# Who stores the expert results: ScalarE's own queue in place of SyncE's, and new places for every queue

## The chip, the cores and the metric

The kernel runs on one core of a Trainium2 chip. The metric is device time in microseconds (us) for one execution of the whole program, inputs in HBM to output in HBM; three executions are behind the median given below.

## The reference

32 sequences of 512 tokens of width 256 go through one Mamba block and its MLP, a layer norm, and then a mixture of 8 experts plus a shared one; a second layer norm ends it. What matters here is the last part:

```python
scores = softmax(xf @ gate_w.T);  _, idx = top_k(scores, 2)
weights = take_along_axis(scores, idx, -1)
y = per expert: (silu(x @ wg.T) * (x @ wu.T)) @ wd.T
routed = sum over a token's two experts of weight * y
out = layernorm(x + routed + shared(x))
```

## The kernel before

**Batches and engines.** The program walks over 32 batches (one sequence each) and three more periods, `b` in the code. Every engine works through one list of instructions in order. In a batch the Mamba scan takes most of the time: VectorE (DVE) runs 64 scans (L1224), ScalarE (ACT) makes the decay factors for each of them two ahead, into two PSUM banks (L750), GpSimd (POOL) multiplies their inputs (L585) and TensorE (PE) transposes their results (L969), which DVE sums with weights (L1240). Around this run the preparation of the next batch (`pre`), and the gate, the MLP and the shared expert of the batch before (`post`).

**Routed rows.** GpSimd scatters each token's row, with its weight as a 257th element, to two places in the HBM table `X_slots`, so that rows of one expert lie together. When a group of batches (6, 6, 6, 6, 4, 2, 1, 1) is complete, DVE works out a table `where` in SBUF: for each tile of 128 rows the row number it begins at and the expert. Two tiles make a pair; pairs 0 to 151 are spread over batches 5 to 30, in 12 slots per batch: 5 or 4 pairs in a batch at first, then 7, 10 and 12, and 8 in batch 30. The last group's 8 pairs have their own code, `last`.

**One pair's way.** SyncE (SP) loads the two experts' weights into `wx[k]` and the rows into `xin[k]`, with k the pair's number modulo 2 (L480 to L490). PE transposes the rows (L1107), ACT copies them out (L837), PE multiplies (L1125), ACT takes a tanh (L842), DVE makes the hidden values (L1368, L1371), PE multiplies again (L1140), and ACT scales the two result tiles into `xin[k]` (L853). Then SP stores both to `Y_slots` at the same row numbers. Before each DMA whose address depends on the data, SP reads the number with `value_load`:

```python
sp.wait_ge(s_yo, (p + 1) * 2)                     # ACT wrote both results of pair p
if before[g] >= 0: sp.wait_ge(s_gathered, ...)    # the table's former rows were read
for i in range(2):
    r = sp.value_load(where[g % 2][0:1, 0, tile + i:tile + i + 1], ...)
    sp.dma_start(Y_slots[g % 2][bass.ds(r, P), :], xin[k][:, i, 0:D]).then_inc(s_Y_out[k], 16)
```

The loads of pair p wait for `s_Y_out[k]` of pair p-2, since they write the same buffers. `finish` later gathers from `Y_slots` for each batch (POOL, L642), normalises it (ACT) and stores it.

**The order.** On each engine the strands (scan, pre, post, experts, results, finish and so on) are generators. `weave` merges them by a written table of places, `AT`: a step of batch b stands at 64 b plus its entry, and the lowest is issued next. SP's strands are the batches' inputs, `B_rows` (L409), the broadcasts `Bbc` for the scan (`B_spread`, L418, four buffers, each waiting until GpSimd is done with its former content), `experts` (the loads), `results` (the stores), `finish` and `last`.

Of the kernel before, what the change touches and what calls it, by code (L numbers as in the profile page):

```python
# [9 lines left out]
def group_sizes(n):  # L10
# [6 lines left out]
    while n:  # L17
# [4 lines left out]
AT = {  # L22
    "ACT_clear": [58.23, 58.23, 58.25, 58.25, 60.69, 60.69, 62.42, 62.42, 62.86, 70.07, 91.79, 94.81, 94.81, 95.76,
        95.89, 96.2, 101.55, 101.55, 101.55],
    "ACT_experts": [124.75, 125.75, 129.08, 130.18, 134.55, 136.08, 137.89, 139.34, 141.67, 141.67, 144.29, 145.62,
        147.34, 149.08, 152.77, 153.29, 159.33, 160.04, 160.86, 162.05, 166.89, 167.48, 170.25, 171.88],
    "ACT_finish": [152.64, 152.64, 152.64, 152.79, 153.07, 153.12, 153.36, 153.36, 155.18, 155.73, 156.96, 157.93,
        167.33, 167.33, 167.96, 167.96, 167.96, 168.52, 168.52, 168.91, 170.14, 170.82, 170.93, 171.03, 193.37,
        193.51, 193.51, 193.86, 199.66, 199.99, 199.99, 199.99, 200.21, 200.21, 200.21, 200.21],
    "ACT_last": [136.01, 137.58, 138.23, 138.31, 138.43, 138.43, 138.43, 138.43, 140, 140.51, 140.51, 142.7, 142.7,  # L30
        142.7, 142.7, 142.7, 143.93, 143.93, 143.93, 143.93, 143.93, 144.04, 144.04, 144.04, 144.04, 147.88, 148.81,
        148.81, 152.33, 154.88, 164.02, 167.57],
    "ACT_post": [59.67, 59.67, 64.96, 69.44, 79.33, 80.25, 80.77, 80.77, 82.16, 82.16, 82.16, 82.16, 82.8, 83.44,
        83.44, 84.7, 85.35, 85.71, 87.26, 87.56, 88.85, 90.21, 97.47, 97.47, 98.66, 98.69, 99.97, 101.17, 102.57,
        102.89, 104.72, 105.69, 109.85],
    "ACT_pre": [-61.77, -61.77, -61.77, -58.5, -58.31, -58.31, -49.46, -48.98, -47.21, -33.7, -33.7, -32.82, -32.38,
        -32.27, -30.87, -25.5, -23.6, -20.88, -19.14, -17, -13.55, -12.39, -10.98, -7.68, -5.62, -2.35],
    "ACT_results": [127.98, 128.73, 131.12, 131.93, 137.03, 137.03, 140.85, 141.1, 143.74, 143.74, 146.2, 146.61,
        150.27, 150.3, 158.46, 158.66, 160.18, 160.83, 165.45, 165.85, 168.76, 169.32, 172.65, 172.65],
    "ACT_scan": [2.32, 2.32, 6.33, 8, 8, 8.52, 8.78, 9.17, 9.17, 10.82, 12.09, 12.09, 14.29, 14.29, 15.76, 15.83,  # L40
# [3 lines left out]
    "ACT_weigh": [8.76, 9.09, 10.64, 11.74, 34.98, 36.17, 36.53, 37.63],  # L44
    "DVE_experts": [127.17, 129.69, 136.27, 139.69, 144.39, 148.41, 149.45, 153.29, 161.06, 162.66, 169.85, 175.15],
    "DVE_last": [129.08, 140.77, 140.77, 140.77, 153.53, 153.53, 158.09, 203.9],
    "DVE_meta": [108.09, 109.36, 110.61, 111.98],
    "DVE_post": [57.6, 62.15, 65.02, 68.32, 69.12, 73.9, 75.44, 75.44, 93.47, 97.9, 98, 98, 98.02, 102.46, 104.09,
        104.09, 104.74, 104.74, 104.98, 105, 105.13, 106.39, 107.33, 108.88],
    "DVE_pre": [-29.64, -26.56, -26.56, -25.13, -25.03, -23.53, -20.37, -19.9, -19.9, -18.38, -18.38, -18.38],  # L50
    "DVE_scan": [3.32, 3.48, 6.82, 7.53, 8.29, 8.29, 8.38, 10.1, 10.7, 11.64, 14.78, 14.86, 17.75, 19.56, 20.14,
# [4 lines left out]
    "DVE_weigh": [16.36, 17.6, 17.6, 19.63, 20.54, 20.54, 20.54, 20.54, 20.54, 20.54, 20.54, 22.81, 23.36, 23.36,  # L56
# [3 lines left out]
    "PE_experts": [122.03, 123.93, 126.2, 128.38, 135.99, 135.99, 139.17, 139.31, 141.28, 141.28, 146.72, 146.82,  # L60
        149.57, 149.57, 152.77, 152.77, 159.71, 161.24, 164.33, 164.59, 168.56, 168.83, 173.68, 174.09],
    "PE_inputs": [121.91, 125.67, 133.2, 137.49, 140.56, 145.8, 148.99, 152.41, 158.77, 164.23, 168.28, 170.67],
    "PE_last": [128.18, 128.18, 128.18, 130.61, 144, 144, 144, 154.96, 160.84, 161.21, 198.92, 198.92, 198.92,
        198.92, 222.27, 247.75, 247.75, 336.97, 357.99, 357.99, 357.99, 357.99, 357.99, 370.12],
    "PE_post": [55.43, 56.65, 56.65, 57.47, 58.38, 59.94, 61.6, 66.95, 67.63, 69.63, 73.15, 74.6, 75.44, 75.98,
        77.21, 79.8, 81.28, 81.6, 81.6, 81.74, 86.07, 86.07, 86.84, 86.84, 86.84, 86.84, 88.16, 88.52, 88.87, 88.87,
        90.27, 90.7, 90.98, 93.38, 93.38, 98.19, 99.97, 100.05, 100.95, 100.99, 102.79, 104.52, 104.52, 105.96,
        106.05, 106.16, 106.26, 109],
# [20 lines left out]
    "SP_experts": [110.03, 122.95, 127.33, 133.34, 144.56, 147.72, 148.88, 158.4, 159.99, 163.15, 164.6, 166.33],
    "SP_finish": [139.78, 160.64, 169.44],  # L90
    "SP_inputs": [-67.65],
    "SP_last": [105.48, 105.79, 115.27, 119.17, 119.17, 119.17, 119.17, 119.29, 119.29, 120.53, 135.17, 135.17,
        135.52, 135.52, 135.52, 147.56, 147.56, 147.56, 147.56, 159.42, 159.42, 159.42, 159.42, 159.42],
# [22 lines left out]
def build(nc, a, out):  # L116
    F32, BF16 = mybir.dt.float32, mybir.dt.bfloat16
    ALU = mybir.AluOpType
    ACT = mybir.ActivationFunctionType
# [61 lines left out]
    with ctx:  # L181
# [199 lines left out]
        def _(sp):  # L381
# [110 lines left out]
            def results():  # L492
                for b in range(PERIODS):
                    for p in pairs_in[b]:
                        if p is None:
                            yield from empty(b, 1)
                            continue
# [977 lines left out]
```

## Time and profile before

| | us |
|---|---|
| median of 3 runs | 5452.79 (5439.62 to 5469.59) |
| the profiled execution | 5453.14 |
| its span on the core | 5451.4 |
| DVE, PE, POOL, ACT busy in the span | 4418.7, 4273.5, 3581.1, 3392.8 |
| granted TensorE clock, mean share of full speed | 0.91 |

"Busy" counts instructions that compute; waits, register instructions and the issue of DMAs are not in it. A row of the timeline gives the start, the duration and, in brackets, how long the engine had been idle before and what ended that. A line that ends in q (SPq, ACTq) is the engine's sequencer, which issues DMAs; "x2" says that two like instructions in a row were merged.

### The profile page before, as it was taken

The page shows a single profiled execution, that of the slowest core. Times are in us where ns is not written, and L with a number is a line of the kernel's source. Part 1 is how long each engine was busy: PE and PEld are TensorE (multiplying, and loading weights), DVE is VectorE, ACT ScalarE, POOL GpSimd, SP SyncE. Part 2 cuts the span into 40 slices and gives each one's busy share as a digit, 9 for nine tenths or more (in the row PEclk, how much of TensorE's full clock was granted, in tenths as well). Part 3 has the DMA queues.
Part 4 walks back from the last instruction along what each step waited for, and adds up shares of the span by engine and source line. Part 5 has one row for each costly group of instructions (what it writes and reads, how often), then busy time and mean ns, then how long its engine had stood idle before and what let it go on. Part 6 is the DMA issues. An engine that isn't in the chain of part 4 may idle for free. (4 is left out here: it accounts for less than half of the span.)

```text
span 5451.4 us, 75865 instructions
## 1 busy us (share of the span) xinstructions
PE 4273.5 (78%) x20928; PEld 2954.8 (54%) x20928; DVE 4418.7 (81%) x6313; ACT 3392.8 (62%) x6338; POOL 3581.1 (66%) x2252
## 2 busy tenths in 40 slices
PE   3777877788888888878887778888878888888873
PEld 2455555455555555555555555555555566555652
DVE  5889988978888887788888788788888888878741
ACT  4666666556666656666666666666667776667633
POOL 4666666656566566666677666677767785677743
PEclk7898898999899999899999899899999999988987
DMA  1122522233333333332332332333334442455555
GB/s 57 61 76 80 136 81 79 81 101 116 107 127 111 107 92 98 89 104 84 88 95 77 97 103 84 87 92 89 94 110 113 125 132 88 141 141 145 155 141 152
DMA packets 357156, 563.53 MB, mean 103 GB/s; under 512 B 40433, under 2 KB 203378, under 8 KB 356610
## 3 DMA queue, kind: packets, MB, share of 16 engines
q1 hardware_dynamic: 253250, 398.07, 24.4%
q0 software_dynamic: 49152, 67.27, 6.1%
q10 hardware_dynamic: 54336, 93.34, 5.1%
q8 instruction: 174, 2.85, 0.2%
q14 instruction: 244, 2.00, 0.1%
HBM read 440.66 MB, written 186.05 MB: 115 GB/s over the span
## 5 line engine op out<-in xcount | busy, mean ns | idle before, releaser
L585 POOL TENSOR_TENSOR dBx<-dtx,Bbc 128x1024 f32<-128x1024 f32 x1024 | 2424.0, 2397 | 749.3 <-DVE hs L1224 721.5
L1224 DVE TENSOR_TENSOR_SCAN hs<-ps,dBx 128x512 f32<-128x512 f32 x2048 | 2397.8, 1208 | 179.7 <-ACT ps L750 132.9
L750 ACT ACTIVATE ps<-dt,A 128x512 f32<-128x512 f32 x2048 | 1389.4, 690 | 598.4 <-DVE hs L1224 538.5
L969 PE MATMUL ps<-ident,hs 128*128 128x128 f32 x8192 | 1325.6, 302 | 366.4 <-DVE acc L1240 186.7
L969 PEld LDWEIGHTS ps<-ident,hs 128*128 128x128 f32 x8192 | 1037.7, 154 | 858.8 <-issue 408.2
L1240 DVE SCALAR_TENSOR_TENSOR acc<-ps,C_tok,acc 128x512 f32<-128x512 f32 x1792 | 1282.0, 740 | 237.1 <-PE ps L969 218.6
L642 POOL DMA_INDIRECT fx<-Y_slots,slots x256 | 403.8, 1577 | 124.8 <-issue 56.7
L618 POOL DMA_INDIRECT X_slots<-xs,slots x256 | 257.1, 1004 | 323.4 <-DVE slots L1356 264.4
L1125 PE MATMUL ps<-xsT,wx 128*128 128x128 f32 x2432 | 339.8, 293 | 99.1 <-ACT xsT L837 99.1
L1125 PEld LDWEIGHTS ps<-xsT,wx 128*128 128x128 f32 x2432 | 317.0, 207 | 130.5 <-issue 127.6
L1213 DVE SCALAR_TENSOR_TENSOR xc<-ps,conv_w,xc 128x511 f32<-128x511 f32 (+2 forms) x384 | 285.5, 744 | 74.3 <-ACT xc L714 65.9
L934 PE MATMUL ps<-xnT,w_in 128*128 128x512 f32 x512 | 274.9, 654 | 75.5 <-DVE xc L1213 74.7
L1368 DVE SCALAR_TENSOR_TENSOR ge<-ge,ps 128x256 f32<-128x256 f32 x152 | 63.4, 417 | 325.2 <-ACT ge L842 322.1
L986 PE MATMUL ps<-xnT,w_in 128*128 128x512 f32 x512 | 316.1, 715 | 0.0
L569 POOL TENSOR_TENSOR dt<-dt,dtx 128x1024 f32<-128x1024 f32 x64 | 152.2, 2378 | 197.4 <-ACT dtx L741 197.4
L1016 PE MATMUL ps<-w_out,xc 128*128 128x256 f32 x1024 | 259.9, 391 | 0.0
L1049 PE MATMUL ps<-w_m,post_tmp 128*128 128x256 f32 x1024 | 252.1, 379 | 0.0
L1032 PE MATMUL ps<-mT,w_m 128*128 128x512 f32 x512 | 240.2, 602 | 15.1 <-ACT mT L793 10.6
L714 ACT ACTIVATE xc<-ps,conv_b,conv_w 128x512 f32<-128x512 f32 x128 | 99.0, 774 | 218.8 <-PE ps L934 216.8
L1140 PE MATMUL ps<-wx,ge 128*128 128x256 f32 x608 | 178.1, 418 | 66.8 <-DVE ge L1371 64.6
L958 PE MATMUL ps<-few 16*128 16x512 f32 x256 | 188.3, 826 | 52.4 <-DVE hs L1224 27.1
L837 ACT ACTIVATE xsT<-ps 128x512 f32<-128x512 f32 x152 | 90.0, 592 | 205.4 <-PE ps L1107 203.0
(210 smaller groups left out, 6090.3 us busy)
## 6 DMA issues: line engine op xcount, KB each, us to landing
Bbc<-B_scratch SPq DMA_DIRECT2D x512, 256.0 KB
wx<-in_experts SPq DMA_DIRECT2D x308, 384.0 KB, 5.3
Y_slots<-zeros ACTq DMA_DIRECT2D x228, 256.0 KB, 3.6
xin<-X_slots SPq DMA_DIRECT2D x308, 128.5 KB, 4.1
Y_slots<-xin SPq DMA_DIRECT2D x308, 128.0 KB
xt<-in_x SPq DMA_DIRECT2D x32, 512.0 KB, 5.6
shared<-xt ACTq DMA_DIRECT2D x32, 512.0 KB
fx<-shared SPq DMA_DIRECT2D x32, 512.0 KB
```

What stands on the lines that cost most here:

```text
L585: pool.tensor_tensor(dBx[u % 3][:], dtx[b % 2][:, 2 * h:2 * h + 2, :], Bbc[g % NBB][:, n % CH:n % CH + 1, :].broadcast_to([P, 2, T]), ALU. ...
L618: pool.indirect_dma_start(out=X_slots[g % 2], out_offset=bass.IndirectOffsetOnAxis(ap=slots[:, b % NKEPT, c, t:t + 1], axis=0), in_=xs[:, ...
L642: pool.indirect_dma_start(out=fx[:, t, :], out_offset=None, in_=Y_slots[g % 2], in_offset=bass.IndirectOffsetOnAxis(ap=slots[:, f % NKEPT, ...
L750: act.activation(psA[s % 2][:], dt[b % 2][:, j, :], ACT.Exp, scale=A[:, j, n:n + 1]).then_inc(s_dA, 1)
L934: i = pe.matmul(bank(b, j)[:], w_in[:, k, j * P:(j + 1) * P], xn[:, k, :], start=(k == 0), stop=(k == KD - 1))
L969: i = pe.transpose(psH[w % 2][:, j * P:(j + 1) * P], hs[(n * CT + j) % NHB][:, t * P:(t + 1) * P], ident[:])
L986: i = pe.matmul(psG[j % 2][:], w_in[:, k, DI + j * P:DI + (j + 1) * P], xn[:, k, :], start=(k == 0), stop=(k == KD - 1))
L1016: i = pe.matmul(psG[q][:, t * D:(t + 1) * D], c[:, k, (2 * q + t) * P:(2 * q + t + 1) * P], w_out[:, k, :], start=False, stop=(k == CT - 1))
L1125: i = pe.matmul(psE[:, o * HALF + m * P:o * HALF + (m + 1) * P], w[:, m, (2 * k + o) * P:(2 * k + o + 1) * P], xsT[:, (m * KD + k) * P:(m ...
L1213: dve.scalar_tensor_tensor(out=c[:, j, s:], in0=bank(b, j)[:, 0:T - s], scalar=conv_w[:, j, NK - 1 - s:NK - s], in1=c[:, j, s:], op0=ALU.m ...
L1224: dve.tensor_tensor_scan(hs[s % NHB][:], psA[s % 2][:], dBx[s // 2 % 3][:, s % 2, :], 0.0, ALU.mult, ALU.add).then_inc(s_scan, 1)
L1240: dve.scalar_tensor_tensor(out=o, in0=psH[w % 2][:], scalar=C_tok[b % 2][:, t, n:n + 1], in1=o, op0=ALU.mult, op1=ALU.add).then_inc(s_weig ...
```

## The change

SP's strand `results` is gone. ACT's strand `results` gets a third step for each pair, in which it waits for its own two result tiles, for the gathers and for the table `where`, reads both row numbers and issues both stores on its own DMA queue:

```diff
@@ sync @@
-            def results():
-                ...
-                        sp.wait_ge(s_yo, (p + 1) * 2)
-                        if before[g] >= 0:
-                            sp.wait_ge(s_gathered, gathers(first[before[g]] + groups[before[g]] - 1))
-                        for i in range(2):
-                            r = sp.value_load(where[g % 2][0:1, 0, tile + i:tile + i + 1], min_val=0, max_val=ROWS - P)
-                            sp.dma_start(Y_slots[g % 2][bass.ds(r, P), :], xin[k][:, i, 0:D]).then_inc(
-                                s_Y_out[k], 16)
...
@@ scalar, results @@
                         for i in range(2):
                             yield b
                             act.wait_ge(s_down_e, p + 1)
-                            act.activation(xin[p % 2][:, i, 0:D], psE[:, i * D:(i + 1) * D], ACT.Copy,
-                                           scale=xin[p % 2][:, i, D:ROW]).then_inc(s_yo, 1)
+                            act.activation(xin[k][:, i, 0:D], psE[:, i * D:(i + 1) * D], ACT.Copy,
+                                           scale=xin[k][:, i, D:ROW]).then_inc(s_yo, 1)
+                        yield b
+                        act.wait_ge(s_yo, (p + 1) * 2)
+                        if before[g] >= 0:
+                            act.wait_ge(s_gathered, gathers(first[before[g]] + groups[before[g]] - 1))
+                        act.wait_ge(s_meta, (g + 1) * NMETA)
+                        for i in range(2):
+                            r = act.value_load(where[g % 2][0:1, 0, tile + i:tile + i + 1], min_val=0, max_val=ROWS - P)
+                            act.dma_start(Y_slots[g % 2][bass.ds(r, P), :], xin[k][:, i, 0:D]).then_inc(s_Y_out[k], 16)
```

Nearly every entry of `AT` is another number, mostly by less than one place in 64. Those that the prediction speaks of (the twelve slots of a batch are the columns; ACT's results now have three entries per slot):

```diff
-    "SP_experts": [110.03, 122.95, 127.33, 133.34, 144.56, 147.72, 148.88, 158.4, 159.99, 163.15, 164.6, 166.33],
-    "SP_results": [124.93, 132.24, 136.86, 145.2, 147.75, 154.41, 158.46, 160.8, 163.86, 164.62, 168.83, 176.47],
+    "SP_experts": [106.86, 108.87, 130.44, 135.81, 143.11, 145.05, 145.81, 150.54, 154.74, 161.01, 161.01, 161.01],
-    "ACT_results": [127.98, 128.73, 131.12, 131.93, 137.03, 137.03, 140.85, 141.1, 143.74, 143.74, 146.2, 146.61,
...
+    "ACT_results": [128.79, 128.88, 129.17, 131.79, 132.06, 134.08, 136.96, 136.96, 137.26, 139.83, 140.55, 140.55,
+        143.32, 143.48, 143.48, 145.66, 146.04, 146.52, 150.26, 150.9, 152.4, 158.66, 158.66, 159.11, 160.25, 160.53,
...
-    "SP_B_spread": [-5.78, -4.69, -4.69, -2.74, 8.16, 8.16, 21.1, 21.46, 22.74, 35.01, 35.03, 35.6, 36.9, 38.27,
-        39.5, 42.35],
+    "SP_B_spread": [-13.16, -2.29, 0.35, 1.28, 10.17, 16.9, 22.83, 22.83, 23.43, 27.24, 27.56, 28.23, 34.68, 34.68,
+        42.58, 42.58],
```

## Rows read from the trace of the kernel before

**Rows 1.** The page: busy us, share of the span, instructions.
```profile
PE 4273.5 (78%) x20928; PEld 2954.8 (54%) x20928; DVE 4418.7 (81%) x6313; ACT 3392.8 (62%) x6338; POOL 3581.1 (66%) x2252
```

**Rows 2.** Timeline: once a batch, the store of its rows (batches 1, 2, 11, 12).
```profile
467.41 0.34 ACTq L825 DMA_DIRECT2D shared<-xt  x1
...
614.35 0.33 ACTq L825 DMA_DIRECT2D shared<-xt  x1
...
2199.07 0.33 ACTq L825 DMA_DIRECT2D shared<-xt  x1
...
2368.04 0.33 ACTq L825 DMA_DIRECT2D shared<-xt  x1
```

**Rows 3.** Waits of the whole span: who for whom, us, times, longest.
```profile
DVE ge L1368 <- ACT ge L842: 322.1, 102, 17.6
...
DVE hs L1224 <- ACT ps L750: 132.9, 176, 4.9
...
PE ps L1107 <- DMA xin<-X_slots: 116.0, 50, 6.4
```

**Rows 4.** Waits of SP's queue, the same columns.
```profile
SPq L505 <- ACT xin L853: 1798.8, 146, 29.8
...
SPq L486 <- DMA Y_slots<-xin: 33.9, 23, 3.2
```

**Rows 5.** Timeline of SP's queue after the second pair of batch 12.
```profile
2257.91 1.82 SPq L506 DMA_DIRECT2D Y_slots<-xin  x2
2259.84 0.37 SPq L519 DMA_DIRECT2D fx<-shared  x1
2261.66 0.35 SPq L488 DMA_DIRECT2D wx<-in_experts  x1
...
2264.37 0.33 SPq L490 DMA_DIRECT2D xin<-X_slots  x1
```

**Rows 6.** Timeline: the third pair of batch 12 on its engines.
```profile
2268.88 1.11 PE L1107 MATMUL ps<-ident,xin 128*128 128x128 f32 x4 [4.48 <-DMA xin<-X_slots]
...
2275.01 0.39 ACT L842 ACTIVATE ge<-ps 128x256 f32<-128x256 f32 x1 [4.39 <-PE ps L1125]
...
2275.43 0.42 DVE L1368 SCALAR_TENSOR_TENSOR ge<-ge,ps 128x256 f32<-128x256 f32 x1 [9.51 <-ACT ge L842]
```

**Rows 7.** Lines L505, L506 and L853: durations ns min/median/max, first and last start us.
```profile
L505 SPq TENSOR_LOAD <-where x304: 262/268/616, 1103.2 to 5327.7; - x152
L505 SPq FUSED_REGOPS  x304: 126/152/159, 1103.5 to 5328.0; - x152
...
L506 SPq DMA_DIRECT2D Y_slots<-xin x304: 108/345/899, 1103.9 to 5328.4; - x152
...
L853 ACT ACTIVATE xin<-ps,xin x304: 452/468/500, 1102.3 to 5326.1; 128x256 f32<-128x256 f32 x152
```

**Rows 8.** Timeline: ACT around the store of batch 12 in rows 2.
```profile
2367.43 0.58 ACT L820 ACTIVATE xt<-ps 128x512 f32<-128x512 f32 x1
...
2368.58 0.69 ACT L750 ACTIVATE ps<-dt,A 128x512 f32<-128x512 f32 x1 [0.57 <-ACT xt L820]
```

**Rows 9.** Timeline: the first pair of batch 12, its results and what follows.
```profile
2237.33 0.84 ACT L853 ACTIVATE xin<-ps,xin 128x256 f32<-128x256 f32 x2 [0.94 <-PE ps L1140]
...
2238.06 0.60 ACT L772 ACTIVATE post_tmp<-ps 128x512 f32<-128x512 f32 x1
...
2238.53 0.70 ACT L750 ACTIVATE ps<-dt,A 128x512 f32<-128x512 f32 x1
...
2238.90 1.44 SPq L506 DMA_DIRECT2D Y_slots<-xin  x2
...
2239.57 1.21 DVE L1224 TENSOR_TENSOR_SCAN hs<-ps,dBx 128x512 f32<-128x512 f32 x1
```

**Rows 10.** Timeline: the results of the third pair of batch 12 and DVE behind.
```profile
2277.86 0.82 ACT L853 ACTIVATE xin<-ps,xin 128x256 f32<-128x256 f32 x2
2278.79 0.69 ACT L750 ACTIVATE ps<-dt,A 128x512 f32<-128x512 f32 x1
...
2280.43 3.44 DVE L1224 TENSOR_TENSOR_SCAN hs<-ps,dBx 128x512 f32<-128x512 f32 x3
```

More of the change, by code:

```diff
@@ L22 @@
 AT = {
[L23 to L35, printed above, removed]
@@ L44 @@
[L44 to L49, printed above, removed]
@@ L62 @@
[L62 to L68, printed above, removed]
@@ L88 @@
-    "SP_behind": [56.54, 231.2, 245.47],
-    "SP_experts": [110.03, 122.95, 127.33, 133.34, 144.56, 147.72, 148.88, 158.4, 159.99, 163.15, 164.6, 166.33],
[L90 to L93, printed above, removed]
-    "SP_results": [124.93, 132.24, 136.86, 145.2, 147.75, 154.41, 158.46, 160.8, 163.86, 164.62, 168.83, 176.47],
+    "ACT_clear": [56.21, 58.95, 58.95, 68.49, 69.32, 69.37, 69.37, 69.37, 82.25, 83, 86.67, 89.37, 92.15, 94.6,
+        95.02, 97.17, 97.17, 97.27, 101.52],
@@ new lines @@
+    "ACT_experts": [124.81, 126.06, 129.12, 129.72, 134.45, 136.53, 138.24, 139.67, 141.86, 141.86, 144.24, 144.61,
+        146.68, 148.4, 152.76, 154.21, 159.25, 160.04, 161.01, 162.77, 166.62, 167.06, 173.35, 176.02],
+    "ACT_finish": [152.79, 152.79, 152.79, 152.88, 153.56, 153.99, 153.99, 154.59, 157, 157.58, 157.61, 158.02,
+        167.13, 167.13, 167.13, 167.24, 167.24, 167.24, 167.29, 168.13, 171.51, 171.51, 172.17, 172.17, 193.9,
+        194.13, 194.15, 194.15, 194.25, 194.25, 194.52, 194.67, 196.68, 196.98, 197.78, 198.38],
@@ new lines @@
+    "ACT_last": [132.1, 133.46, 133.46, 134.59, 137.01, 137.01, 137.01, 137.01, 137.01, 137.01, 137.3, 143.06,
+        143.06, 143.06, 144.27, 144.27, 145.53, 145.53, 145.53, 145.53, 145.53, 146.05, 146.51, 146.51, 146.51,
+        146.51, 150.38, 150.38, 150.38, 152.27, 160.61, 168.86],
+    "ACT_post": [57.19, 60.53, 63.96, 68.82, 79.06, 79.06, 80.25, 80.45, 81.44, 81.55, 81.55, 81.55, 83.78, 83.78,
+        84, 84, 85.03, 85.54, 87.39, 87.9, 88.87, 89.41, 98.69, 98.93, 99.07, 99.54, 100.13, 101.13, 102.76, 102.98,
+        104.23, 105.46, 109.76],
@@ new lines @@
+    "ACT_pre": [-64.89, -64.51, -62.13, -61.82, -56.61, -55.85, -54.9, -54.9, -33.92, -33.92, -33.73, -33.36, -32.45,
+        -32.39, -29.58, -25.56, -24.03, -20.5, -19.31, -16.12, -14.48, -14.48, -12.86, -9.54, -6.91, -2.6],
+    "ACT_results": [128.79, 128.88, 129.17, 131.79, 132.06, 134.08, 136.96, 136.96, 137.26, 139.83, 140.55, 140.55,
+        143.32, 143.48, 143.48, 145.66, 146.04, 146.52, 150.26, 150.9, 152.4, 158.66, 158.66, 159.11, 160.25, 160.53,
+        160.98, 165.78, 166.21, 166.21, 168.41, 168.41, 168.57, 179.22, 180.55, 180.55],
@@ new lines @@
+    "ACT_scan": [3.44, 3.72, 6.83, 7.89, 7.89, 8.66, 9.34, 10.25, 10.7, 11.03, 11.8, 12.24, 14, 14, 15.64, 16.07,
[4 rows of a table added]
+    "ACT_weigh": [8.81, 10.36, 11.73, 11.73, 35.71, 36.61, 36.94, 39],
+    "DVE_experts": [127.11, 128.81, 137.25, 139.58, 143.68, 146.82, 149.87, 153.19, 160.76, 165.04, 168.75, 176.56],
+    "DVE_last": [116.91, 141.07, 144.19, 172.7, 176.19, 197.29, 197.29, 257.14],
+    "DVE_meta": [108.84, 108.84, 109.01, 109.01],
+    "DVE_post": [59.34, 62.81, 63.95, 69.83, 69.83, 73.71, 75.1, 76.03, 90.43, 94.55, 97.71, 97.71, 97.91, 102.66,
+        103.05, 104.39, 104.39, 104.39, 104.39, 104.39, 104.68, 104.77, 105.23, 108.88],
@@ new lines @@
+    "DVE_pre": [-28.28, -26.93, -26.93, -25, -24.66, -24.57, -22.74, -22.63, -20.64, -18.95, -18.74, -18.37],
+    "DVE_scan": [4.78, 5.12, 9.04, 9.04, 9.04, 10.17, 11.06, 11.06, 11.06, 12.42, 12.42, 12.64, 16.22, 17.73, 17.73,
[4 rows of a table added]
+    "DVE_weigh": [12.44, 16.19, 16.79, 17.43, 20.95, 20.95, 21.1, 21.1, 21.19, 21.52, 21.52, 22.67, 24.3, 25.09,
[3 rows of a table added]
+    "PE_experts": [122.38, 123.98, 126.54, 127.05, 134.42, 134.52, 138.46, 138.69, 141.56, 142.9, 146.61, 146.61,
+        149.24, 149.68, 153.96, 154.14, 159.17, 161.26, 164.58, 164.58, 168.7, 168.89, 177.55, 177.55],
@@ new lines @@
+    "PE_inputs": [121.83, 126.24, 132.67, 136.68, 140.42, 146.13, 147.89, 151.83, 158.49, 164.11, 168.37, 174.02],
+    "PE_last": [134.39, 152.19, 163.43, 163.43, 164.85, 174.18, 174.18, 174.68, 178, 198.27, 198.27, 230.16, 287.33,
+        288.61, 302.39, 376.79, 428.57, 431.04, 431.04, 431.04, 431.04, 431.04, 458.4, 460.46],
+    "PE_post": [55.59, 55.59, 56.08, 56.51, 59.56, 60.18, 62.16, 67.89, 68.09, 69.24, 72.57, 75.13, 75.53, 76.14,
+        77.5, 78.92, 80.97, 80.97, 80.97, 82.41, 85.89, 85.89, 86.65, 86.74, 86.87, 87.01, 87.42, 87.51, 88.5, 89.06,
+        90.71, 91.39, 91.52, 91.99, 93.16, 97.06, 98.98, 99.81, 101.12, 101.39, 102.52, 104.52, 104.62, 105.37,
+        105.47, 105.59, 106.43, 109.89],
@@ new lines @@
+    "PE_pre": [-33.06, -32.81, -30.5, -28.56, -24.46, -23.79, -22.65, -22.65, -21.07, -20.49, -16.18, -15.55, -14.68,
+        -14.15, -13.68, -13.68, -12.04, -11, -8.85],
+    "PE_results": [124.6, 127.78, 136.23, 139.3, 144.81, 146.69, 150.4, 155.42, 162.63, 165.9, 169.53, 178.69],
+    "PE_turn": [7.63, 8.69, 10.1, 11.15, 11.25, 12.01, 16.33, 16.83, 18.92, 18.92, 18.92, 20.36, 21.12, 21.38, 21.64,
[4 rows of a table added]
+    "POOL_finish": [140.28, 140.75, 142.97, 142.97, 148.92, 148.92, 148.92, 148.92, 154.45, 154.53, 156.88, 159.26,
+        160.43, 160.56, 162.86, 162.86, 167.25, 167.25, 167.36, 167.9, 172.72, 173.04, 175.05, 176.53, 177.55,
+        177.55, 177.55, 187.48, 195.93, 196.98],
@@ new lines @@
+    "POOL_post": [82.23, 82.63, 98.32, 104.42, 104.79, 104.79, 104.79, 104.79, 105.67, 105.79, 106.04, 106.04],
+    "POOL_pre": [-58.95, -39.54, 0.21, 6.09],
+    "POOL_scan": [4.85, 7.2, 7.81, 7.94, 8.42, 13.08, 13.08, 13.08, 16.07, 17.43, 18.58, 26.09, 26.2, 27.93, 27.93,
+        27.93, 27.93, 28.62, 33.22, 33.95, 36.18, 36.9, 37.78, 39.72, 41.92, 44.5, 45.98, 46.33, 47.27, 48.61, 48.61,
+        49.23],
+    "SP_B_rows": [-16.35],
+    "SP_B_spread": [-13.16, -2.29, 0.35, 1.28, 10.17, 16.9, 22.83, 22.83, 23.43, 27.24, 27.56, 28.23, 34.68, 34.68,
+        42.58, 42.58],
@@ L95 @@
+    "SP_behind": [10.08, 151.18, 287.95],
+    "SP_experts": [106.86, 108.87, 130.44, 135.81, 143.11, 145.05, 145.81, 150.54, 154.74, 161.01, 161.01, 161.01],
+    "SP_finish": [136.91, 159.96, 165.82],
+    "SP_inputs": [-74.09],
+    "SP_last": [104.51, 104.51, 104.51, 106.44, 106.44, 106.44, 106.44, 114, 114, 114.58, 123.87, 135.87, 149.39,
+        149.39, 149.39, 149.39, 149.39, 162.86, 162.86, 162.86, 162.86, 162.86, 162.86, 165.87],
 }
@@ L490, in experts @@
                             sp.dma_start(xin[k][:, i, :], X_slots[g % 2][bass.ds(r, P), :]).then_inc(s_xin[k], 16)
-            def results():
[L493 to L497, printed above, removed]
-                        g, k = group_of_pair[p], p % 2
-                        tile = 2 * (p - pairs_to[g]) + tiles[g]
-                        yield b
-                        sp.wait_ge(s_yo, (p + 1) * 2)
-                        if before[g] >= 0:
-                            sp.wait_ge(s_gathered, gathers(first[before[g]] + groups[before[g]] - 1))
-                        for i in range(2):
-                            r = sp.value_load(where[g % 2][0:1, 0, tile + i:tile + i + 1], min_val=0, max_val=ROWS - P)
-                            sp.dma_start(Y_slots[g % 2][bass.ds(r, P), :], xin[k][:, i, 0:D]).then_inc(
-                                s_Y_out[k], 16)
             def finish():
@@ L522, in _ @@
                   (experts(), AT["SP_experts"]),
-                  (results(), AT["SP_results"]), (finish(), AT["SP_finish"]), (last(), AT["SP_last"]))
+                  (finish(), AT["SP_finish"]), (last(), AT["SP_last"]))
             sp.wait_ge(s_stored, 16 * NB)
@@ L847, in results @@
                         if p is None:
-                            yield from empty(b, 2)
+                            yield from empty(b, 3)
                             continue
+                        g, k = group_of_pair[p], p % 2
+                        tile = 2 * (p - pairs_to[g]) + tiles[g]
                         for i in range(2):
```

22 lines of the change are left out of this document (removed), and 29 rows, old and new, of the table AT.

## The prediction

> **What bounds the kernel now.** I began with the page's busy times: DVE computes in 81% of the span, ACT in 62% [rows 1]. The share says little by itself, so I next read the length of a batch off its one regular mark, the store of its rows. With no expert work a batch takes 614.35 - 467.41 = 146.9 us; batch 12, with 5 pairs, takes 2368.04 - 2199.07 = 169.0 us [rows 2]. The reader is to see that 5 pairs cost 22 us, though they put only 5 x 2 x 0.42 = 4.2 us of work on DVE. The list of waits says where the rest is: DVE's largest wait is for a pair's tanh, 322.1 us in 102 times, and it is the end of a chain of single steps (rows loaded, transposed, copied, multiplied, tanh) whose first link is itself late 50 times, by 116.0 us in all: PE stands before the transposes until `xin` has landed [rows 3]. DVE also waits 132.9 us for ACT's decay factors.
>
> Then the waits of SP's queue, for why the loads are late. SP stood 1798.8 us, 146 times, before a store, waiting for ACT's results; for the buffer that a load needs, the one thing it must wait for, it stood 33.9 us [rows 4]. So SP is always at the store in time (the store gains nothing), but what is queued behind it is held. The timeline shows one case whole: the stores of the second pair go out at 2257.91, a load for `finish` follows, and only at 2261.66 to 2264.70 are the third pair's weights and rows requested [rows 5]. PE has stood 4.48 us when it can transpose at 2268.88, the tanh is done at 2275.40, and DVE starts at 2275.43 after 9.51 idle us [rows 6]. The remaining 5.0 us of DVE's idle time are the chain itself and stay.
>
> **What is removed.** With the stores gone from SP, the third pair's load stands, by its place 143.11, behind the fifth `Bbc` of the next batch (its place 10.17 is 138.17 there), which waits only for GpSimd's products of the batch's first state; the second pair's (130.44) stands behind the fourth (129.28), free at the end of the batch before. Both are ten or more us ahead of PE. The wait for the load should therefore vanish. What it is worth to DVE is, pair by pair, the smaller of PE's wait for the load and DVE's wait for the tanh of that pair: 1.50 and 4.48 us for the second and third pair of batch 12, nothing for the other three. Read so over all 152 pairs (the 50 waits of the row in [rows 3]) it makes 61 us in the twelve batches of 5 pairs, 0 in the six of 4, 9 in the four of 7, 8 in the two of 10, 4 in that of 12 and 13 in batch 30 and the tail: **-95 us**. The bounds are 0, if another link is as late, and -116.
>
> The Trainium skill's page "DMA: Bandwidth & Descriptors" (section "Issuing engines are not separate DMA queues") says that issuing from another engine saves only the issuing sequencer's time. The trace agrees that the transfers gain nothing, but it puts the saving not at the two issues but at the 1798.8 us wait ahead of them.
>
> **What is added on ACT.** The step is two value loads, two issues and a wait for its own results, and ACT's list is in order: every activation behind it stands still. The store in the profile shows the size: a TENSOR_LOAD of 0.27 us, register work of 0.15 and an issue of 0.345 [rows 7]. SP issues the first DMA 2238.90 - 2238.17 = 0.73 us after ACT's second result ends and is through 1.44 us later [rows 9]. Then ACT has to start again: at its own store in batch 12 the activation ends at 2368.01, the issue takes 2368.04 to 2368.37, and the next activation starts at 2368.58 [rows 2, 8], so 0.03 us for waiting on its own semaphore and 0.21 to restart. Together 0.73 + 1.44 + 0.21 = 2.4 us. ACT has never read a register from SBUF in this trace. From below I take 1.8 us (no overhead between the listed instructions: 2 x (0.27 + 0.15 + 0.345) + 0.03 + 0.21); from above, were the load on this engine as slow as the slowest one here, 0.616 us [rows 7], 2.4 + 2 x 0.35 = 3.1 us. I take 2.4: the sequencers issue a DMA in the same time (0.33 and 0.345), so I expect the same of the loads. The other two waits (gathers, table) are met long before and cost a few hundredths.
>
> 152 x 2.4 = 365 us of ACT, but ACT is idle 38% of the time. How much reaches DVE I read pair by pair: delay the instruction behind the second result by 2.4 us, let ACT's idle gaps eat into it, and take the most by which a decay factor is then later than DVE's start on it. First pair of batch 12: L772 and the factor at 2238.53 follow at once, the factor is ready at 2239.23 and DVE takes it at 2239.57 [rows 9], so 2.4 less 0.3, 2.1 us, reach DVE. Third pair: the factor at 2278.79 is ready at 2279.48 and used at 2280.43 [rows 10]; 1.4 us. The second pair's costs 2.4, the fourth's 0.2, the fifth's 0: 6.1 us in the batch. Read so over the 304 activations of L853 (152 pairs, the first at 1102.3, the last at 5326.1 [rows 7]) it makes 73 us in the batches of 5, 27 in those of 4, 28 in those of 7, 18 in those of 10, 9 and 2 in the last two: **+158 us** (109 with 1.8 us a pair, 231 with 3.1).
>
> **What the new places do to that.** In the first slot ACT's results stand at 128.79 and 128.88 and the stores at 129.17, behind one more decay factor, the batch's last; behind it DVE still has weighted sums to do (0.74 us each), so the stall is covered there: -2.1 us x 25 batches = -53 us. In the third slot (the second of 5 pairs) two squares of `pre` have moved between the results and the stores, with the next decay factor behind both. The squares are 2 x 0.69 us; DVE, which has one scan less to do there than before, waits longer, by about 2.2 us in the 15 batches that use this slot behind the first: +33 us. The other slots have their stores right behind the results, as I counted them. The remaining entries shift single steps past each other; I find nothing in them to charge or credit, and give them +-30 us.
>
> **The sum**, against the profiled execution (5453.14 us, span 5451.4, the median of the runs is 5452.79): -95 + 158 - 53 + 33 = +43 us, so **5496 us**.
>
> **Rivals.**
> 1. *The stall is small or covered* (ends faster). The mechanism of the loads is as above and -95 us come in full; with 1.8 us a pair, 109 reach DVE, and less the 53 of the first slot and without the charge of the third it is -95 + 109 - 53 = -39: 5414 us; were two thirds of the stalls covered by the new order, it is -95 + 53 = -42 with 2.4 us a pair, 5411, and with both -95 + 36 = -59, 5394. For it: ACT's 38% idle. Against it: of the five pairs of batch 12 three have a decay factor behind them with 1.0 us of cover or less. It decides once less than 95 us of stalls reach DVE, 0.6 us a pair.
> 2. *Both cancel* within 27 us: 5453. It needs the gain as read and 95 us of stalls, about the lower price with one of the two changes of place.
> 3. *The loads were not the late link* : in the third slot DVE comes late by the store's stall, the `post` steps on PE behind it come late too, and PE's transposes start when they did. Then the gain in the batches of 5 is gone (61 us): 43 + 61 = +104, 5557 us. For it: the stall of the second pair sits right ahead of the third pair's chain. Against it: 4.48 us is more than 2.4.
> 4. *The value load is dear on ACT*, 3.1 us a pair: -95 + 231 - 53 + 33 = +116, 5569 us. The Trainium skill's page "DMA: Bandwidth & Descriptors" (section "Latency and other measured facts") gives a tensor_load a floor of about 600 ns. The trace has it at 0.27 us on SP, so the rule fails there, and no row shows ACT.
>
> **How the numbers follow.** My forecast 0.38, rival 1 0.28, rival 2 0.16, rival 3 0.11, rival 4 0.07. About 0.5% (27 us) is what a measurement can tell here. The range goes from a little beyond rival 1's far end to a little beyond rival 4: 5385 to 5590; alone my forecast would have 5450 to 5545. A part of the forecast (below 5480) and of rival 2 falls within 0.5%: faster 0.29, same 0.22, slower 0.49.
>
> **What would show it.** Right: SP's waits for L853 are gone and PE's 116.0 us before L1107 fall under 30; the row of DMA issues names ACTq for `Y_slots<-xin`; ACT shows gaps of about 2.4 us behind L853; DVE's wait for ACT's factors (132.9 us) grows by about 100; a batch of 5 pairs takes 169 to 173 us. Wrong: the gap is under 1.5 us (rival 1) or over 3 (rival 4); DVE's wait for the tanh stays at 322 though the loads are early (rival 3); or the sum of DVE's waits falls, with the new places as the reason.

## The result and the profile after

The changed kernel takes 5472.56 us in the median of 8 runs (5466.96 to 5492.04), the kernel before 5445.19 us (5431.60 to 5469.59, 8 runs). The ratio is 1.0049, with a 95% interval of 1.0028 to 1.0070: 27 us slower, small but outside the noise. The profiled execution took 5477.96 us. Two executions of the experiments below stand far outside, one of e3 (14271 us at a granted clock of 0.54) and one of e4 (12771 us at 0.31): the medians given count them, the ratios do not.

The page of the changed kernel, its busy times and its row of DMA issues for the stores:

```profile
PE 4394.6 (80%) x20928; PEld 3057.7 (56%) x20928; DVE 4409.4 (81%) x6313; ACT 3387.0 (62%) x6338; POOL 3582.4 (65%) x2252
...
Y_slots<-xin ACTq DMA_DIRECT2D x304, 128.0 KB
```

Its list of waits (who for whom, us, times, longest):

```profile
DVE acc L1234 <- PE ps L963: 337.2, 293, 4.3
DVE hs L1218 <- ACT ps L734: 218.3, 205, 4.2
...
DVE ge L1362 <- ACT ge L826: 148.7, 77, 12.6
...
PE ps L1101 <- DMA xin<-X_slots: 13.6, 9, 4.6
```

and that of SP's queue:

```profile
SPq L419 <- POOL dBx L569: 3063.1, 405, 24.4
...
SPq L487 <- DMA Y_slots<-xin: 381.1, 50, 18.5
```

Against [rows 3, 4]: SP's 1798.8 us before the stores are gone; it now stands where it has to, before `Bbc` and, for 381.1 us instead of 33.9, before the buffer of a load. PE's wait for `xin` fell from 116.0 to 13.6 us, DVE's wait for the tanh from 322.1 to 148.7. Two of DVE's waits grew instead: for ACT's factors, from 132.9 to 218.3 (the prediction had about 100 more), and for PE's transposed states, from 218.6 to 337.2, for which the prediction has no term. Batch 12 takes 168.8 us; the prediction had 169 to 173, and it was 169.0 before.

The third pair of batch 12, which had the longest stretch in [rows 6], in the timeline of the changed kernel:

```profile
2247.95 0.60 PE L1101 MATMUL ps<-ident,xin 128*128 128x128 f32 x4
...
2251.67 0.38 ACT L826 ACTIVATE ge<-ps 128x256 f32<-128x256 f32 x1 [2.48 <-PE ps L1119]
...
2252.08 0.42 DVE L1362 SCALAR_TENSOR_TENSOR ge<-ge,ps 128x256 f32<-128x256 f32 x1 [4.37 <-ACT ge L826]
```

PE no longer waits for the load, and DVE is idle for 4.37 us instead of 9.51: the chain itself is left, as forecast (5.0 us). What the store costs ACT stands in the durations of its two lines (ns min/median/max, first and last start):

```profile
L847 ACTq TENSOR_LOAD <-where x304: 275/282/610, 1099.9 to 5350.2; - x152
L847 ACTq FUSED_REGOPS  x304: 152/152/175, 1100.4 to 5350.7; - x152
...
L848 ACTq DMA_DIRECT2D Y_slots<-xin x304: 338/343/550, 1100.8 to 5351.1; - x152
```

The value load takes 0.28 us on ACT and 0.27 on SP [rows 7]. The gap, from the end of a pair's second result to the next activation behind its stores, is 2.2 us in the median of the pairs; I had taken 2.4. "Stall" below is this gap.

### The profile page after: what moved, and what is told of

It reads as the page before. It is cut to its first block and busy times, and to the rows that moved or that the text cites. A ratio compares the mean times of both kernels' runs of the same rounds, so it can differ in the third digit from the quotient of the medians.

```text
span 5476.1 us, 75887 instructions
## 1 busy us (share of the span) xinstructions
PE 4394.6 (80%) x20928; PEld 3057.7 (56%) x20928; DVE 4409.4 (81%) x6313; ACT 3387.0 (62%) x6338; POOL 3582.4 (65%) x2252
## 5 line engine op out<-in xcount | busy, mean ns | idle before, releaser
L1218 DVE TENSOR_TENSOR_SCAN hs<-ps,dBx 128x512 f32<-128x512 f32 x2048 | 2402.4, 1207 | 276.4 <-ACT ps L734 218.3
L963 PE MATMUL ps<-ident,hs 128*128 128x128 f32 x8192 | 1416.5, 315 | 596.8 <-DVE acc L1234 390.7
L963 PEld LDWEIGHTS ps<-ident,hs 128*128 128x128 f32 x8192 | 1086.5, 160 | 1146.8 <-DVE acc L1234 644.2
L1234 DVE SCALAR_TENSOR_TENSOR acc<-ps,C_tok,acc 128x512 f32<-128x512 f32 x1792 | 1279.7, 736 | 348.8 <-PE ps L963 337.2
L980 PE MATMUL ps<-xnT,w_in 128*128 128x512 f32 x512 | 314.6, 726 | 0.0
L928 PE MATMUL ps<-xnT,w_in 128*128 128x512 f32 x512 | 258.0, 619 | 5.7 <-DVE xc L1207 4.8
L952 PE MATMUL ps<-few 16*128 16x512 f32 x256 | 231.7, 1002 | 21.9 <-ACT dt L720 11.9
L1043 PEld LDWEIGHTS ps<-w_m,post_tmp 128*128 128x128 f32 x1024 | 197.2, 196 | 39.4 <-issue 14.3
L1010 PEld LDWEIGHTS ps<-w_out,xc 128*128 128x128 f32 x1024 | 197.6, 197 | 26.8
```

The costliest lines, as they stand in the source:

```text
L963: i = pe.transpose(psH[w % 2][:, j * P:(j + 1) * P], hs[(n * CT + j) % NHB][:, t * P:(t + 1) * P], ident[:])
L980: i = pe.matmul(psG[j % 2][:], w_in[:, k, DI + j * P:DI + (j + 1) * P], xn[:, k, :], start=(k == 0), stop=(k == KD - 1))
L1010: i = pe.matmul(psG[q][:, t * D:(t + 1) * D], c[:, k, (2 * q + t) * P:(2 * q + t + 1) * P], w_out[:, k, :], start=False, stop=(k == CT - 1))
L1043: i = pe.matmul(psG[q][:, t * D:(t + 1) * D], post_tmp[:, k, (2 * q + t) * P:(2 * q + t + 1) * P], w_m2[:, k, :], start=False, stop=(k == ...
L1218: dve.tensor_tensor_scan(hs[s % NHB][:], psA[s % 2][:], dBx[s // 2 % 3][:, s % 2, :], 0.0, ALU.mult, ALU.add).then_inc(s_scan, 1)
L1234: dve.scalar_tensor_tensor(out=o, in0=psH[w % 2][:], scalar=C_tok[b % 2][:, t, n:n + 1], in1=o, op0=ALU.mult, op1=ALU.add).then_inc(s_weig ...
```

## The experiments

Three questions: what each part (loads earlier, stores on ACT, new places) is worth alone; whether the time added is ACT's stall; and what in the places gives back what. Each ratio is to the kernel before, with its 95% interval, and 0.01 of it is 54 us. A difference of two ratios is uncertain by 0.003 to 0.004, 15 to 20 us. Where the batches of one profiled execution are compared, a batch is the stretch between two stores of rows, as in [rows 2].

**e1, stores on ACT in the old places.** The changed kernel with every table of the kernel before.

```diff
-    "ACT_results": [128.79, 128.88, 129.17, 131.79, ...],
+    "ACT_results": [127.98, 128.73, 128.73, 131.12, ...],   # third entry = second
```

> The change of engine alone: ScalarE stores, every place as before, the store step right behind the second result. Theory A (the stall of 2.3 us a pair on ScalarE reaches VectorE for 158 us in all, the earlier loads give 95 back): +63 us, ratio 1.010 to 1.014, VectorE's wait for the factors up by over 100 us, granted clock about 0.91. Theory B (the stall is mostly covered; what costs is the new places, through a lower granted clock, 0.88 against 0.91): ratio 0.985 to 0.995.

5586.4 us, 1.0267 [1.0234, 1.0300]. Its waits:

```profile
DVE acc L1232 <- PE ps L961: 271.1, 296, 4.9
DVE hs L1216 <- ACT ps L732: 262.0, 237, 4.9
DVE ge L1360 <- ACT ge L824: 244.2, 103, 16.0
```

The tanh wait is 78 us shorter, the wait for factors 129 us longer and that for PE 53 us. The move by itself costs 145 us, more than both expectations; the new places are worth 119.

**e2, new places with the stores on SP.** A store stands at its old place, or ahead of the load that needs its buffer, whichever is first.

```diff
+                            store(p - 2)
                             sp.wait_ge(s_Y_out[k], stores(p - 2, k))
```

> The new places alone: SyncE stores again, at its old places (and ahead of a load that needs the buffer), everything else at the new ones. Theory A: no stall on ScalarE; the loads stand partly behind the stores again; ratio 0.985 to 1.000. Theory B: the new places bring the lower clock, 0.88 to 0.89, with them; ratio 1.003 to 1.012.

5531.66 us, 1.0163 [1.0130, 1.0195], above both expectations. PE waits for `xin` 38 times, and SP stands behind its stores again:

```profile
SPq L505 <- ACT xin L859: 1509.3, 122, 33.0
```

So the new places aren't better as such: in this mixture, with the stores at SP's old places, they cost 89 us, with the stores on ACT they give 119. They fit the engine that stores.

**e3, loads ahead of the stores, on SP.** The kernel before, but a pair's loads are always issued right before SP waits for the previous pair's results.

```diff
+                        if p + 1 < P0 and group_of_pair[p + 1] == g:
+                            loads_of(p + 1)
                         sp.wait_ge(s_yo, (p + 1) * 2)
```

> Kernel before, places as before, stores still on SyncE; only the loads of the next pair are issued ahead of the wait for this pair's results. It has the gain and not the stall. Theory A: -95 us, ratio 0.980 to 0.987, TensorE's wait for xin under 20 us, granted clock may fall a little. Theory B in its other form (a TensorE that waits less is granted a lower clock, which takes the gain back): clock 0.89 or less and ratio 0.990 to 1.000.

5465.25 us, 1.0047 [1.0027, 1.0067], above both expectations. It was ahead of the kernel before by 52 us at the end of batch 22, the last with 4 pairs (3946.28 against 3998.36), and lost it afterwards, where pairs come more densely and "right before the previous store" is later than the load's old place. That is a fault of the edit, and the next one mends it.

**e5, the loads alone.** As e3, but a load keeps its old place where that comes first.

```diff
+                        loads_of(p)          # at the old place too; issued once
```

> Kernel before with SyncE storing; a pair's loads stand at their old place or ahead of the stores of the pair before, whichever comes first. The run with the loads ahead won 52 us up to batch 22 and lost them again from batch 23 on. Theory A (in the crowded batches it had moved some loads behind their old place, and the stores behind them): the loss there goes, ratio 0.983 to 0.991. Theory B (in crowded batches the earlier loads have no value): ratio 1.000 to 1.006, the same course over the batches.

5414.75 us, 0.9954 [0.9935, 0.9973]: the fastest kernel of the study, faster than the kernel before and the changed one. It lies between the two expectations and meets neither. Its waits:

```profile
DVE ge L1377 <- ACT ge L851: 231.9, 103, 15.8
DVE acc L1249 <- PE ps L978: 225.5, 290, 3.6
DVE hs L1233 <- ACT ps L759: 163.8, 179, 4.9
...
PE ps L1116 <- DMA xin<-X_slots: 29.0, 13, 6.7
```

DVE's wait for the tanh fell by 90 us, almost the 95 of the prediction, but the time by only 25: 31 us came back as waits for ACT's factors, 7 as waits for PE. I read this so: a pair that is through sooner lets DVE ask sooner for factors that ACT has not made.

The course over the batches shows more than the sum. At the end of batch 22 e5 is 47 us ahead of the kernel before (3951.68 against 3998.36), at the end of the span only 36. Behind batch 22, where a batch has 7 to 12 pairs, PE's wait for `xin` fell from 46.6 to 20.8 us, and the tanh wait hardly moved. This is DVE's wait in that stretch, before and in e5:

```profile
DVE ge L1368 <- ACT ge L842: 116.2, 36, 17.6
```

```profile
DVE ge L1377 <- ACT ge L851: 113.1, 41, 15.8
```

So of the 90 us all but 3 lie in batches 5 to 22. In the crowded batches a load that comes sooner did not bring the tanh sooner, and the time there is 11 us longer. Which link is late there, no run separates.

Against e5, with the loads free in both, e1 is 3.1% slower: the stores on ACT cost 171 us.

**e4 and e8, a shorter stall.** ACT reads both row numbers ahead of the wait for the first result, where it is idle; the stores are then two issues. e4 is the changed kernel so, e8 is e1 so.

```diff
+                            if i == 0:
+                                act.wait_ge(s_meta, (g + 1) * NMETA)
+                                rows = [act.value_load(where[g % 2][...tile + c...]) for c in range(2)]
                             act.wait_ge(s_down_e, p + 1)
                             act.activation(xin[k][:, i, 0:D], ...)
...
-                            r = act.value_load(where[g % 2][...])
+                            r = rows[i]
```

> Changed kernel, but ScalarE reads both row numbers ahead of the wait for the first result, where it often waits anyway; only the two issues stay behind the results, so the gap there should fall from 2.2 to about 1.0 us. Theory A: some 60 to 90 us less than the changed kernel, ratio to before 0.988 to 0.996. Theory B: within 0.3% of the changed kernel, 1.002 to 1.008.

> ScalarE stores, old places, and both row numbers read ahead of the first result, so that the gap is 1.1 us shorter. Theory A (in the old places a stall reaches VectorE for half of its length and more): 85 to 130 us less than the old places alone, ratio 1.003 to 1.011. Theory B (what costs in the old places is not the length of the stall but its being there): under 50 us less, 1.018 to 1.027.

e4: 5434.55 us, 0.9989 [0.9971, 1.0007], as long as the kernel before, and between its two expectations. e8: 5486.38 us, 1.0092 [1.0061, 1.0123], as its theory A has it. The gap behind the second result falls to 1.2 and 1.1 us. Over 152 pairs e8 takes away 1.07 x 152 = 163 us of stall and gains 0.0175, 95 us; e4 takes away 1.0 x 152 = 152 us and gains 0.006, 33 us. A microsecond of stall between 1.1 and 2.2 us costs 0.58 us in the old places and about 0.2 in the new.

**e7, a longer stall.** The changed kernel with each row number read three times.

```diff
+                            act.value_load(where[g % 2][...])
+                            act.value_load(where[g % 2][...])
                             r = act.value_load(where[g % 2][...])
```

> Changed kernel, each row number read three times: the stall grows by 4 reads, some 1.9 us a pair, 290 us of ScalarE in all. Theory A (a stall reaches VectorE for more than half of its length once the gap is over 2 us): +120 to +220 us on the changed kernel, ratio 1.028 to 1.045. Theory B (the new places cover most of it, as the 0.22 us per us of the early reads suggests): +40 to +90 us, ratio 1.012 to 1.021.

5764.64 us, 1.0595 [1.0562, 1.0628], far above both expectations. The gap is 4.42 us, 2.22 us or 337 us in all more, and the time grows by 297: 0.88 us for each. The wait of `hs` for ACT's factors shows the larger part, 386.5 us against 218.3; the tanh wait grew by another 65:

```profile
DVE hs L1220 <- ACT ps L734: 386.5, 217, 6.5
```

With e4 this gives the shape in the new places: from 1.2 to 2.2 us of stall they cover four fifths of what is added, from 2.2 to 4.4 us only an eighth. Below 1.2 us no run shows it.

**e6, the first slot alone.** e1 with the first slot's store behind the batch's last decay factor.

```diff
-    "ACT_results": [127.98, 128.73, 128.73, ...],
+    "ACT_results": [127.98, 128.73, 129.1, ...],
```

> ScalarE stores, old places, and one entry of 2 moved: in the first slot of a batch the store step stands behind the batch's last decay factor, as in the changed kernel. Theory A (this one move covers a stall in each of 25 batches): 53 us less than with the old places alone, ratio 1.015 to 1.019. Theory B (the gain of the new places is spread over many steps): within 15 us of the old places alone, 1.024 to 1.029.

5518.9 us, 1.0150 [1.0117, 1.0183]: one entry of a table is worth 0.0117, 64 us. The forecast was 53, and this is theory A.

**e10, both cures in the old places.** e8 with the same entry at 129.1.

> The places of the kernel before, stores on ACT, row numbers read ahead (1.0092 of before without the next edit), and the first slot's store put behind the last decay factor of the batch (worth 64 us with the long stall: 1.0267 to 1.015). Theory A (the two edits add, the second in the measure of the stall that is left, 1.2 us of 2.2): 30 to 50 us less than 1.0092, 0.999 to 1.004. Theory B (the early reads have taken up the same slack): less than 15 us more, 1.006 to 1.010.

5464.44 us, 1.0030 [1.0010, 1.0050]: 34 us less than e8, as theory A has it. The two add, the second in the measure of the stall that is left (1.1 of 2.2 us, 34 of 64 us).

**e11, where the rest of the places' gain lies.** e1 with all of SP's tables from the changed kernel.

> Stores on ACT, the places of the kernel before on ACT, PE, DVE and POOL, and all of SP's places from the new kernel (1.0267 of before with SP's old places). The question is where the 50 us lie that the new places gave beside the first slot. Theory A (in SP's order: loads and broadcasts stand where nothing holds them): 30 to 50 us less, 1.017 to 1.021 of before. Theory B (SP's order is free once the stores are off it, the 50 us lie in the order of the computing engines): 1.024 to 1.029.

5563.72 us, 1.0217 [1.0194, 1.0241]: 27 us less than e1. It falls between the two expectations, nearer to the first: about half of the 50 us is SP's order, the other half lies elsewhere.

**e12, the squares put back.** The changed kernel with two entries of one table.

```diff
-    "ACT_pre": [-64.89, -64.51, -62.13, -61.82, -56.61, -55.85, -54.9, -54.9, -33.92, ...],
+    "ACT_pre": [-64.89, -64.51, -62.13, -61.82, -56.61, -55.85, -49.46, -48.98, -33.92, ...],
```

> The new kernel with the two squares of the preparation, which stand between the third slot's results and its stores, put back behind the decay factors that follow. Theory A (the term of the prediction is right, 2.2 us in 15 batches): 33 us less, 0.998 to 1.000 of before. Theory B (what the squares delay there is in time anyway, or costs the same where they go): 1.003 to 1.007, no change against the new kernel.

5500.13 us, 1.0103 [1.0080, 1.0125]: slower by 29 us. Neither expectation allowed that sign. The timeline of ACT in batch 6 shows why the squares cost nothing where they were. The changed kernel, with the squares (L663) between results and stores:

```profile
1277.00 0.84 ACT L839 ACTIVATE xin<-ps,xin 128x256 f32<-128x256 f32 x2 [1.46 <-PE ps L1134]
1277.72 0.51 ACT L663 ACTIVATE dtx<-xt,less_pre 128x256 f32<-128x256 f32 x1
...
1278.22 0.50 ACT L663 ACTIVATE dtx<-xt,less_pre 128x256 f32<-128x256 f32 x1
1278.56 0.35 ACTq L848 DMA_DIRECT2D Y_slots<-xin  x1
1278.62 0.19 ACT L663 ACTIVATION_READ_ACCUMULATOR dtx<-xt,less_pre 128x1 f32 x1
1279.61 0.34 ACTq L848 DMA_DIRECT2D Y_slots<-xin  x1
1280.06 1.30 ACT L734 ACTIVATE ps<-dt,A 128x512 f32<-128x512 f32 x2 [1.25 <-issue]
```

and e12, without them:

```profile
1281.88 0.84 ACT L838 ACTIVATE xin<-ps,xin 128x256 f32<-128x256 f32 x2 [1.38 <-PE ps L1133]
1283.44 1.41 ACTq L847 DMA_DIRECT2D Y_slots<-xin  x2
1284.96 1.30 ACT L733 ACTIVATE ps<-dt,A 128x512 f32<-128x512 f32 x2 [2.23 <-issue]
```

From the end of the second result to the next factor it is 1280.06 - 1277.84 = 2.22 us with the squares and 1284.96 - 1282.72 = 2.24 without. The sequencer hands the squares to the engine and goes on to the reads and issues while they run; they end at 1278.81, before even the second store is issued. Here 1.1 us of work between the results and the stores is free inside a stall of 2.2 us, and I had charged it.

That does not yet give the 29 us. In the profiled executions 22 of e12's 23 us on the changed kernel arise in batches 5 to 8 (6.0, 6.9, 5.2 and 3.6 us), and from there to the end the two keep level within a few us, though e12 has the squares outside the stall in all 14 batches that use the third slot and prepare another batch. So the loss is not a fixed price for each batch; what the squares delay in those four is not shown.

**e9, the stores later.** e4 with the store step 1.3 places later in all slots but the first, so that more work stands ahead of it.

```diff
-    "ACT_results": [128.79, 128.88, 129.17, 131.79, 132.06, 134.08, 136.96, 136.96, 137.26, ...],
+    "ACT_results": [128.79, 128.88, 129.17, 131.79, 132.06, 135.38, 136.96, 136.96, 138.56, ...],
```

> The new kernel with the row numbers read ahead (as in the run that did only that: 0.9989 of before) and, in every slot but the first, the store step put 1.3 places later, so that one to three more activations stand between the second result and the two stores. Theory A (the stall costs most where a decay factor stands right behind it, and a factor ahead of it covers it, as in the first slot): DVE gets its next factor in time, 20 to 40 us less than with the row numbers read ahead alone, 0.990 to 0.996 of before; DVE's wait for ACT's factors falls from about 218 towards 150. Theory B (with the new places and the shorter stall there is no cover left to gain, the stall only moves to the next factor): 0.997 to 1.002.

5469.2 us, 1.0043 [1.0027, 1.0059]: 29 us slower than e4, a miss of both expectations. Its waits:

```profile
DVE acc L1234 <- PE ps L963: 353.2, 264, 6.4
...
DVE ge L1362 <- ACT ge L824: 173.6, 77, 13.6
DVE hs L1218 <- ACT ps L732: 167.9, 179, 3.5
...
PE ps L1101 <- DMA xin<-X_slots: 35.9, 9, 5.5
```

and SP's:

```profile
SPq L485 <- DMA Y_slots<-xin: 490.0, 59, 17.4
```

In e4 the wait of `hs` was 175.8 us, so only 8 us of it were gained; SP's wait for the buffer was 369.2 us and is 490.0. A store that goes out later frees its buffer later, the next but one load is late, and PE's wait for `xin` is at 35.9 us again, from 9.7 in e4. DVE's wait for PE grew by 30 us, from 323.0. I read the second as coming from the first; this store has a price on either side.

## Why the prediction came out as it did

**The balance.** Taken apart by e5, e1 and the result: loads earlier -25 us, stores on ACT +171, new places -119, together +27. The prediction had -95, +158 and -20, together +43. The signs and the largest term are right, and the sum is 16 us off only because two misses of 70 and 99 us nearly cancel. That is luck: the sum was better than its terms. (5472.56 is 23 us below the 5496 of the forecast, but 8 of these are its base, 5453.14, against the 5445.19 that eight runs gave.)

The same terms by stretches, in us, read from one profiled execution of each kernel at the end of batch 22 and of the span, with the prediction's terms beside them (the first slot counted in 18 and 7 batches, the third in 12 and 3):

| | batches 5 to 22 | predicted | from batch 23 | predicted |
|---|---|---|---|---|
| loads earlier (before to e5) | -47 | -61 | +11 | -34 |
| stores on ACT (e5 to e1) | +107 | +100 | +55 | +57 |
| new places (e1 to changed) | -63 | -11 | -38 | -8 |
| together | -3 | +28 | +27 | +15 |

The changed kernel is level with the kernel before at the end of batch 22 (3995.79 against 3998.36). All that it loses, it loses in the crowded batches behind.

**The loads, -95: the mechanism was right up to batch 22, the term mis-sized.** SP's waits before the stores went to nothing in the changed kernel and PE's from 116.0 to 13.6, as forecast. The step that failed is the taking of a shortened wait for a shortened time: pair by pair I took the smaller of two waits, and did not ask what DVE would stand before next. Up to batch 22 that cost little, 47 us against 61, with 29 us more of waiting for ACT's factors, which are made two ahead (69.0 before, 97.8 in e5). In the crowded batches, for which the reading has 34 us, an earlier link of it failed: PE waited 26 us less for `xin`, but the tanh came only 3 us sooner in all, and e5 loses 11.

**The stall, +158: right, +171.** It is 2.2 us a pair instead of 2.4, with more of it reaching DVE. In the profiled executions e1 falls behind e5 by 107 us up to the end of batch 22 and by 55 after it; the pair-by-pair reading has 73 + 27 = 100 and 57 (its parts add up to 157). This reading, delay minus the idle time behind it, is what held best.

**The first slot, -53: right, -64** in the old places.

**The third slot, +33: wrong in sign, -29.** The failing step is that "two squares between the results and the stores" were added to the stall. They ran inside it (and stand there in 14 batches, not 15). The 1.1 us of squares in 14 batches could explain 15 of the 29 us, but the loss of e12 is not spread like that; where it comes from stays open.

**"The remaining entries +-30": -27 by SP's order, and a miscount.** The prediction counts the stores of all other slots right behind their results. In the trace of the changed kernel 29 of them are not: 20 have one of the scan's decay factors in between, 14 of these from batch 23 on. That is the arrangement that was worth 64 us in the 26 batches of the first slot, and no run tests it for these 20. So the sum of the three pieces that were tested, -64 - 29 - 27 = -120, which nearly meets the -119 measured in all, leaves nothing for it. They were taken in different surroundings (the first and third in old places), and the agreement may be luck.

**The rivals.** Rival 4 (a dear value load) is out: the row shows 0.28 us in 304 loads, with one execution's longest at 0.61. The Trainium skill's page "DMA: Bandwidth & Descriptors" (section "Latency and other measured facts") and its floor of about 600 ns for a tensor_load don't agree with this trace: the medians are 0.27 us on SP's queue and 0.28 on ACT's. Rival 3 (the loads not the late link) is out for the batches of 5 pairs, of which it speaks: DVE's 9.51 us became 4.37. From batch 23 on its outcome is what e5 shows, a load that comes sooner and a tanh that does not, though no run shows its mechanism. Rival 1's mechanism, a stall covered by the new order, is half true: the new places give back 119 of 171 us, but the loads give 25 and not 95. Rival 2, that both cancel within 27 us, is met just at its edge, with other sizes: the gain is not as read, and 171 us reach DVE and not 95. The +27 measured are nearer to the +43 of the forecast than to nothing.

**What stays open.** The wait of DVE for PE's transposed states rose by 119 us (218.6 to 337.2), in e2 to 335.3, in e4 to 323.0, while e1, e5, e8 and e11, all with old places on the computing engines, have 225 to 271. Of the 119 us 81 lie in batches 5 to 22, where the changed kernel is not slower. It goes with the places, not with the store. At the same time the granted clock is lower: the page's row of tenths, before and after,

```profile
PEclk7898898999899999899999899899999999988987
```

```profile
PEclk7888888899999889888889888899888889988986
```

with a mean of 0.910 before and 0.877 after. At the two levels of 2.4 and 1.2 GHz that is 2 x 0.09 x 5451 = 981 us at the lower before, and 2 x 0.123 x 5476 = 1347 after. PE's own rows, before and after, show the length of one transpose (busy, mean ns | idle before):

```profile
L969 PE MATMUL ps<-ident,hs 128*128 128x128 f32 x8192 | 1325.6, 302 | 366.4 <-DVE acc L1240 186.7
```

```profile
L963 PE MATMUL ps<-ident,hs 128*128 128x128 f32 x8192 | 1416.5, 315 | 596.8 <-DVE acc L1234 390.7
```

Whether the longer wait is this clock, or PE's new order in front of it, no run tells apart: kernels with the new places on PE alone or on ACT alone weren't tried. Two signs against a large part for the clock in the time: the first four batches behind the first store, which have no pairs, take 146.4 to 146.9 us before and 146.8 after, at a clock of 0.91 and 0.88; and batches 5 to 22 take 2934 us in both, at 0.93 and 0.89.

## What to carry to other kernels

A pair of DMAs with addresses read from memory costs a computing engine 2.2 us in its own list, or a little over one when the addresses are read earlier, and what that is worth is decided by what stands around it: put finished work of the engine between the wait's cause and the store (it runs under the reads), read the addresses where the engine is idle anyway, and keep the store early enough for the buffer it frees. Before moving a blocking store to another engine, try moving what is queued behind it: here ordering the loads ahead of the store on the old queue gave 25 us, while the moved store took 171 and needed new places everywhere to come back to +27. A wait that vanishes is an upper bound: read what the waiting engine stands before next. And look at the course over the stages before explaining a sum: here all of the loss lies in the crowded batches.

## What the runs showed of the hardware

- ScalarE's sequencer runs ahead of its engine: squares issued before a value load and a DMA execute while these are being read and issued (1.1 us hidden in 2.2, the changed kernel against e12), whereas activations behind them wait.
- A pair of stores with addresses read on the spot takes ScalarE 2.2 us, with addresses read earlier 1.1 to 1.2 us (e1 against e8, the changed kernel against e4).
- In the profiled executions the granted TensorE clock went with the order of the program and not with the engine that stores: 0.902 to 0.909 with the old places and stores on ACT (e1, e6, e8), 0.91 in the kernel before; 0.875 to 0.883 with the new (the changed kernel, e2 with stores on SP, e4, e12), and 0.864 in e7 with its longer stall; always 20928 matmuls.
